# GpSimd takes the steps of the reciprocal root, and one group of ten transposes for rotated queries and keys

## The reference, cut to what matters

```python
q = _rmsnorm(einsum('bsd,ed->bse', x, Wq).reshape(..., 32, 128), q_norm_w)
k = _rmsnorm(einsum('bsd,ed->bse', x, Wk).reshape(..., 8, 128), k_norm_w)
v = einsum('bsd,ed->bse', x, Wv)
q = _rope(q, pos); k = _rope(k, pos)
k_all = concatenate([cached 512 keys, k]); v_all = concatenate([cached 512 values, v])
scores = einsum('bqhd,bkhd->bhqk', q, repeat(k_all, 4)) * SCALE
probs = softmax(where(valid, scores, -1e30))
out = x + einsum('bse,de->bsd', einsum('bhqk,bkhd->bqhd', probs, repeat(v_all, 4)), Wo)
# _rmsnorm(t, w) = t * rsqrt(mean(t * t) + EPS) * w
```

## Time and profile before

| | |
|---|---|
| median of three runs | 1390.99 us |
| profiled execution | 1386.9 us, of which the span from first to last instruction 1385.3 us |
| mean granted TensorE clock | 0.996 |
| PE busy | 1360.1 us (98% of the span) |
| DVE busy | 1018.7 us (74%) |
| ACT busy | 804.9 us (58%) |
| POOL busy | 451.2 us (33%) |
| chain that ended last | PE 88%, DVE 4%, issue 4%, ACT 3%, DMA 1% |

### The profile page before, as it was taken

The page is one execution under the profiler, slowest core; times in us unless marked ns, Lnnn a source line. Parts: engine busy times, 40 slices in busy tenths (PEclk is TensorE's granted clock), DMA queues, the critical chain, the costliest instruction groups (busy, mean ns, idle before and its releaser), DMA issues.

```text
span 1385.3 us, 26742 instructions
## 1 busy us (share of the span) xinstructions
PE 1360.1 (98%) x7308; PEld 1155.9 (83%) x7308; DVE 1018.7 (74%) x2602; ACT 804.9 (58%) x1887; POOL 451.2 (33%) x480
## 2 busy tenths in 40 slices
PE   6999999989999999999999999999999999999998
PEld 5888888878888888888888888888888888888887
DVE  4532345868888787887887878888888788888886
ACT  5631334346666657766666577666666776565554
POOL 4000000345332225642333366322322752222221
PEclk9999999999999999999999999999999999999999
DMA  8211214382333344433333454333334443333321
GB/s 293 80 61 46 72 43 127 94 284 80 77 76 76 77 136 137 108 86 78 78 78 76 137 133 108 85 77 81 90 81 141 129 112 98 78 76 76 76 54 31
DMA packets 146643, 135.93 MB, mean 98 GB/s; under 512 B 92816, under 2 KB 111632, under 8 KB 146320
## 3 DMA queue, kind: packets, MB, share of 16 engines
q1 hardware_dynamic: 127616, 83.87, 22.1%
q0 software_dynamic: 11584, 33.82, 10.2%
q10 hardware_dynamic: 7376, 17.45, 3.3%
HBM read 118.15 MB, written 16.91 MB: 97 GB/s over the span
## 4 chain that ended last, share of the span: by engine, by line
PE 88%; DVE 4%; issue 4%; ACT 3%; DMA 1%; ACTq 0%; DVEq 0%
PE bank L1407 17%; PE wide L1478 14%; PE tail L1445 14%; PE tail L1534 11%; PE wide L1439 7%; PE wide L425 4%; PE bank L1428 4%; PE wide L493 3%; PE bank L425 2%; PE tail L425 2%; PE wide L552 2%; PE bank L552 1%; PE bank L493 1%; PE tail L1501 1%; ACT prT L1602 1%
## 5 line engine op out<-in xcount | busy, mean ns | idle before, releaser
L1610 ACT ACTIVATE pr<-pr,nm,q_scale 128x640 f32<-128x640 f32 x256 | 236.2, 923 | 92.1 <-DVE nm L1789 90.3
L1786 DVE CUSTOM_DVE_ANT_0 pr<-wide,bias 128x640 f32<-128x640 f32 x256 | 210.1, 821 | 88.3 <-issue 88.3
L1445 PE MATMUL tail<-prT,vt 128*128 128x512 f32 x960 | 249.8, 401 | 0.0
L1207 POOL TENSOR_TENSOR tick<-tick 128x1 f32<-128x1 f32 x126 | 31.9, 253 | 571.1 <-PE wide L1478 502.9
L1445 PEld LDWEIGHTS tail<-prT,vt 128*128 128x128 f32 x960 | 173.0, 188 | 33.1 <-DVE prT L1771 0.8
L1534 PE MATMUL tail<-woT,oT 128*128 128x512 f32 x768 | 198.4, 402 | 1.0 <-DVE oT L1810 1.0
L1765 DVE TENSOR_TENSOR prT<-wide,prT 128x1024 fp32r<-128x1024 f32 x128 | 156.8, 1225 | 53.9 <-ACT prT L1602 50.0
L1602 ACT CAST prT<-wide 128x1024 fp32r<-128x1024 f32 x128 | 129.9, 1015 | 68.2 <-PE wide L1439 36.1
L1534 PEld LDWEIGHTS tail<-woT,oT 128*128 128x128 f32 x768 | 137.1, 188 | 33.7 <-issue 6.9
L1478 PE MATMUL wide<-kT,qT 128*128 128x320 f32 x512 | 162.1, 317 | 0.5 <-DVE mx L1786 0.5
L1478 PE MATMUL wide<-kT_low,qT 128*128 128x320 f32 x512 | 158.9, 310 | 0.0
(11 more groups left out here) (238 smaller groups left out, 2520.0 us busy)
## 6 DMA issues: line engine op xcount, KB each, us to landing
w_ring<-pair_weights SPq DMA_DIRECT2D x80, 256.0 KB, 4.5
k_raw<-k_pages SPq DMA_DIRECT2D x512, 32.0 KB, 2.8
v_raw<-v_pages SPq DMA_DIRECT2D x512, 32.0 KB, 1.7
spread<-one_over_denominators ACTq DMA_DIRECT2D x32, 512.0 KB, 4.5
xTb<-x_transposed POOLq DMA_DIRECT2D x31, 512.0 KB, 4.9
rope<-rope_tables SPq DMA_DIRECT2D x31, 256.0 KB, 2.6
out<-y POOLq DMA_DIRECT2D x31, 256.0 KB, 4.0
w_raw<-w_gate_up SPq DMA_DIRECT2D x10, 512.0 KB
```

Source lines behind the costliest of these rows:

```text
L1445: last = nc.tensor.matmul(tail[g][:, :], vt[v_part][:, j, g * D:(g + 1) * D], prT[p_part][:, j, :], start=(j == v_part == p_part == 0), st ...
L1610: ac.activation(pr[h][:, :], pr[h][:, :], ACT.Exp, bias=nm[:, h:h + 1], scale=q_scale[:, 0, head(h)], accum_out=den[:, h:h + 1]).then_inc( ...
L1786: v.tensor_tensor_reduce(halves(pr[h][:, :]), scores, halves(bias[:, :]), 1.0, -3.0e38, ALU.add, ALU.max, mx[:, h:h + 1]).then_inc(s_sfree, 1)
```

## The change

The steps of `newton` leave DVE for POOL. There they are four instructions a step instead of three, twelve in a turn, each of which waits for the one before by a semaphore. `root_begin` stays on DVE and now makes half of the mean, so that the step is y (1.5 - t). The keys are scaled (`scale_keys`) once POOL has ended the last step.

PE makes 18 output products, then all ten transposes, then the last 6 output products. The second queries' transposes go to half of `wide[1]` in place of `bank[1]`; ACT copies them from there, and the second head's scores wait until DVE has taken the low part. On DVE the first `low` moves behind the rotation of the second queries, and the third ahead of the mask.

In turns with "next" the Newton steps stand behind the split of the first four weight chunks on POOL, and the keys are scaled behind the rotation of the second queries. In the first turn the Newton steps stand behind the four DMAs of tokens.

```diff
-    FRONT, BACK = (3, 3), (1, 0)
+    FRONT, BACK = (3, 2), (1, 0)
...
+        def newton(u):
+            half_x, y_, t_ = var[:, :], rs[:, :], nt[:, :]
+            at = Count(s_root, u * NROOT)
+            def then(ins):
+                at.inc(ins)
+                pool.wait_ge(s_root, at.value())
+            pool.wait_ge(s_step, u * NSTEP + ROOTED)
+            for i in range(NEWTON):
+                then(nc.gpsimd.tensor_tensor(t_, y_, y_, ALU.mult))
+                then(nc.gpsimd.tensor_tensor(t_, t_, half_x, ALU.mult))
+                then(nc.gpsimd.tensor_tensor(t_, prime[:, 18:19].to_broadcast([P, NH]), t_, ALU.subtract))
+                last = nc.gpsimd.tensor_tensor(y_, y_, t_, ALU.mult)
...
@@ GpSimd, turn
                     nc.gpsimd.dma_start(out[i], x_tok[:, i, :]).then_inc(s_init, 16)
+            if extra != "next":
+                newton(u)
             share_room(u, share is not None)
             if extra == "next":
                 pool.wait_ge(s_step, u * NSTEP + TURNED)
                 low_weights(own, 0, KT)
                 first = KT
+                newton(u)
...
@@ TensorE, turn
                 output(0, REP)
-            if front:
-                pe.wait_ge(s_step, n * NSTEP + TURNED)
-                transposes(1, [ra[:, i, :] for i in range(REP)])
             if back:
                 output(REP, REP // 2)
             if front:
-                pe.wait_ge(s_rope, n * G + 1 + FIRST)
+                pe.wait_ge(s_step, n * NSTEP + TURNED)
+                transposes(1, [ra[:, i, :] for i in range(REP)])
+                pe.wait_ge(s_rope, n * G + 2 + FIRST)
                 transposes(0, [ra[:, REP + i, :] for i in range(G)])
+                pe.wait_ge(t_free[1], n * G + FIRST)
...
+                for i in range(REP):
+                    last = nc.tensor.transpose(wide[1][:, i * P:(i + 1) * P], ra[:, REP + G + i, :], ident[:, :])
+                last.then_inc(s_q1t, 1)
             if back:
                 output(REP + REP // 2, REP // 2).then_inc(s_y, 1)
             if front:
-                pe.wait_ge(s_rope, n * G + 2 + FIRST)
-                transposes(1, [ra[:, REP + G + i, :] for i in range(REP)])
...
                 for h in range(HP):
-                    if h == REP:
-                        pe.wait_ge(c_free[1], rotated + FIRST)
+                    if h == 1:
+                        pe.wait_ge(s_q1free, n + 1)
                     score(h)
...
@@ ScalarE, turn
-                high(1, 3, qT[:, 1, :], bank[1][:, :])
+                act.wait_ge(s_q1t, n + 1)
+                ac.copy(qT[:, 1, :], wide[1][:, 0:REP * S]).then_inc(s_high, 1)
...
@@ VectorE, turn
                 if extra == "next":
                     root_begin()
-                newton()
+                if not back:
+                    scale_keys()
             if back:
                 normalise(1)
-            if front:
-                newton()
+                if front and extra != "next":
+                    scale_keys()
             if back:
                 low_values(1)
...
             if front:
-                newton()
-                keys = ra[:, REP:REP + G, :]
-                v.tensor_tensor(keys, keys, rs[:, REP:REP + G]...).then_inc(s_rope, 1)
-                rotate(REP + G, REP, ((REP + G, REP, 0),),
-                       lambda: low(1, 1, qT_low[:, 0, :], bank[1][:, :], qT[:, 0, :])).then_inc(s_rope, 1)
-                low(2, 0, kT_low[:, :, L:NK], ...)
+                rotate(REP + G, REP, ((REP + G, REP, 0),)).then_inc(s_rope, 1)
+                if extra == "next":
+                    scale_keys()
+                low(1, c_free[1], qT_low[:, 0, :], bank[1][:, :], qT[:, 0, :])
+                low(2, c_free[0], kT_low[:, :, L:NK], ...)
+                low(3, s_q1free, qT_low[:, 1, :], wide[1][:, 0:REP * S], qT[:, 1, :])
                 mask_keys()
                 scales()
-                low(3, 1, qT_low[:, 1, :], bank[1][:, :], qT[:, 1, :])
```

47 lines of the change are left out of this document (27 added, 20 removed).

## The result

The changed kernel takes 1396.08 us, the median of nine runs (1394.9 to 1401.24), beside 1390.57 us for the kernel before in the same comparison (nine runs, 1387.59 to 1392.68): 5.5 us more, a ratio of 1.0055, 95% interval 1.004 to 1.007. The forecast was 6.0 us more.

A forecast was written before the change was run, and what follows sets the result against it. PE, busy 1360.1 of 1385.3 us, was taken to bound the kernel. The terms 3.4 + 2.9 + 1.5 + 0.1 - 1.9 = +6.0 us on 1390.99 gave about 1396.9 us, range 1391.5 to 1401.5.

The forecast's parts named there:

- the four places: Loop turns 1.9 us gained; turns with "out" 2.9, turns with "next" 1.5 and first turn 3.4 us lost.
- the floor: PE's stretch from first output product to first score: 6.6 us without waiting, at most 0.2 us less per loop turn.
- the steps were not long: Rival "much slower": Newton instructions of 0.5 us on POOL make PE wait, +30 us, 1427 us; chance 0.06.
- Steps on POOL, 12 x 0.30 = 3.6 us: Twelve Newton instructions on POOL per turn, 0.22 + 0.08 us each, 3.6 us together; bounds 1.7 and 8.8.
- First turn +3.4: Newton steps wait behind POOL's token DMAs, keys scaled from 307.0, first score 3.4 us late; bounds 2.5 and 4.5.
- Loop turns, 0.08 each, the keys' low part late next: 24 loop turns gain 0.08 us each, 1.9 together; the wait for the rotation goes, `kT_low` is late next.
- "Next", 3 x 0.5: Three turns with "next" lose 0.5 us each, POOL's last steps waiting for DVE's rotation; 1.5 together, bounds 0 and 2.7.
- "Out", 3 x 0.95: Three turns with "out" lose 0.95 us each, ACT's weight chunks delaying the keys' copy; 2.9 together, bounds 1.8 and 3.9.
- The step that failed: On DVE in loop turns: third `low`, mask and scales end by 714.6, hidden before the first head's scores at 714.8.
- the rival "not slower": Loop turns reach the floor and gain 4.8 us, extras at lower bounds; sum 0 to +3, 1391 to 1393.8 us; chance 0.23.
- By what would it show: Expected trace signs: rotation ended near 4.4 us after first output product; stretch near 7.5 in "out", 7.4 in "next".

The follow-up runs named there:

- after_dvefirst: The change, with only the first turn's Newton steps left on DVE; 1394.64 us beside 1386.65 for the kernel before, ratio 1.0058.
- mask_first: The change, with mask and scales again ahead of the third `low` on DVE; 1398.38 us, ratio 1.005 to the kernel before.
- values_first: The change, with POOL's value split ahead of its weight parts in turns with an extra; 1394.79 us, ratio 1.0066 to the kernel before.
- after_again: The change, unedited, timed once more beside the kernel before; 1399.2 us beside 1388.88, ratio 1.0077.

## Why the prediction was right, and where not

The forecast was a loss of 6.0 us: 5.5 by the medians of that comparison. The mechanism was right in the four places that the forecast named, and its rivals were not: the loop turns did not reach the floor, and the steps were not long. By the turns, though, the loss is 10.3 us (9.9 with what stands behind the last score), because a fifth place was missed. The agreement of the medians is in part luck of the starts. Point by point:

- *Steps on POOL, 12 x 0.30 = 3.6 us*: 3.32, 0.28 from start to start. Right.
- *First turn +3.4*: +3.68 measured, of which `after_dvefirst` takes back 3.3. Keys at 310.65 with the first projection 3.87 us later than before, so 306.78 on the clock of before, for 307.0. Right. The low clock cost next to nothing more. What `after_dvefirst` leaves, 0.4 us, is the keys' copy, which waits for transposes that now stand behind the second queries' rotation.
- *Loop turns, 0.08 each, the keys' low part late next*: the stretch lost 0.07 and DVE shows the 1.17 us of waiting for ACT. The mechanism is right for the stretch. The period from score to score lost only 0.04, and the sum, 1.6 us in 21 turns in place of 1.9 in 24 (the three behind "out" are below), came near by other terms: 0.5 us in 15 turns, 0.8 in the five of the third pair, which no row of the forecast showed, and 0.3 in the second turn, which is the clock's.
- *"Next", 3 x 0.5*: 0.28 each. The exclusion of POOL and DVE is there as forecast: four instructions drawn out by 1.0 us, where the forecast had the root at 543.3 instead of 542.3. It came cheaper because the twelve took 3.32 us and not 3.6, and because PE started 0.06 us behind the scaled keys (550.69 to 550.75), not 0.14. The Trainium skill (SBUF — State Buffer, "SBUF: two separate sides") says that whichever starts first has the shared port for its whole instruction; all four rows agree, since each ends just behind DVE's.
- *"Out", 3 x 0.95*: 1.35 each, by the sums of the three (104.30 for 100.26 us), 4.0 us for 2.9. The chunks cost 0.57 of it, less than the 0.85 I took; 0.08 of the difference is the wait behind `kT_low`, which is 0.06 us there and not 0.14. The rest, most of which `mask_first` takes back, comes from "next" and was not in the sum.
- *The step that failed*: "The third `low` (about 713.2 to 713.9), mask and scales follow on DVE until 714.6, and the first head's scores are ready at about 714.8, so they stay hidden". I asked who on PE waits for the scales, and not who else does. POOL does, in the six turns with an extra, and where the third `low` has to wait for ACT the scales wait with it. It cost nothing in the sum. The three turns behind "out" lost 3.3 us (104.85 for 101.52), of which `mask_first` gives back 2.7; of the 4.0 us in the "out" turns it gives back 2.1.
- *A slip in the rival "not slower"*: its lower bounds add up to 0 only with 0.5 for "next", whose lower bound was 0. The chances don't hang on it.
- *By what would it show*: the rotation ended 4.2 us after the first output product (4.4 said), the stretch in "out" was 7.25 (7.5), in "next" 7.19 (7.4).

## What to carry to other kernels

Where two instructions change places on an in-order engine, list for each who waits for it on every other engine, in each kind of turn. An instruction that moved behind a waiting one takes that wait along, and passes it to whoever it releases, here with the loss one turn later. When an engine is relieved, ask first what ends together with the chain that it is on: here two chains ended together, and neither of two edits gained anything in the loop turns alone while both made the kernel 0.4% faster. The distance between the same instruction of successive turns shows 0.1 us where timed runs show 3; look at all turns of a kind, though, since a median hides a group that differs. When two executions of one program differ, compare the rows of the first instructions before explaining the rest.

## What the runs showed of the hardware

- On POOL a chain of dependent two-input instructions of 128x10, with a semaphore after each, runs at 0.28 us from start to start, 0.20 to 0.22 each; on DVE such a chain runs at 0.20, 0.17 each (`before`, first turn). Twelve on POOL take 3.32 us, nine on DVE 1.8. The Trainium skill (GPSIMD Engine Reference, "Engine selection") gives about twice for two-input work; here it is 1.4 times an instruction, and 1.8 times for the whole root, as POOL needs four instructions a step.
- A DVE `tensor_scalar` of 128x10 with one input in SBUF was held for the length of a POOL cast: 1.24 us for 0.17 (`values_first`). I had counted only instructions with two SBUF inputs as open to that. The Trainium skill (SBUF — State Buffer, "SBUF: two separate sides") lists DVE's two-port mode beside them; whether this instruction was in that mode no run here shows.
- From the end of the `low` that the first score waits for to its start it takes 0.31 to 0.33 us in the loop turns of four kernels, where the forecast took the 0.14 of the transposes behind the rotation. It is not the price of a semaphore: in the turns outside the loops the same score starts 0.05 to 0.06 us behind the same `low` (587.56 to 587.62 in "out", 314.67 to 314.73 in the first turn). The loop turns have register instructions there that the others lack; that they take the rest is not shown.
- The first gather that POOL issues took 1.22 us in four profiles and 3.54 to 3.62 in eight, also in two executions of one program (`after_again`).
